# A fused adaLN block on one core: the quantizer's slots by a table, and the engines' lists of steps placed anew

## What is computed

```python
mod = (silu(c) @ wmod)                      # shifts and scales sa, ca, ga, sb, cb, gb per batch
h = layernorm(x) * (1 + ca) + sa
x = x + ga * attn(h, Wq, Wk, Wv, ...)       # decayed sums over all 1024 rows of a batch, per head
h = layernorm(x) * (1 + cb) + sb
gate = fp4(h) @ fp4(w_gate).T
y    = fp4(h) @ fp4(w_up).T
f = silu(gate) * y                          # 352 columns
x = x + gb * (fp4(f) @ fp4(w_down).T)

def fp4(x):                                 # blocks of 16 along the last dimension
    scale = max(max(abs(xb)) / 6, 1e-12)
    return nearest(GRID, abs(xb / scale)) * sign(xb) * scale
```

## Time and profile before

| what | value |
|---|---|
| median of 3 runs | 199.48 us (198.5 to 200.17) |
| the profiled execution's own time | 199.69 us |
| its span (first to last instruction) | 197.7 us |
| PE busy | 184.5 us (93%), 1022 matmuls |
| DVE, POOL busy | 161.1 us, 160.9 us (81% each) |
| ACT busy | 133.8 us (68%) |
| granted TensorE clock | 1.00 in every stretch |

### The profile page before, as it was taken

One profiled execution on the slowest core, in us unless ns is written; L12 is line 12 of the kernel. 1 busy time (PEld: TensorE's weight loads), 2 busy tenths in 40 slices (PEclk: granted clock), 3 DMA queues, 4 the chain that ended last, 5 costly groups with the idle time before them and its releaser, 6 DMA issues.

```text
span 197.7 us, 3626 instructions
## 1 busy us (share of the span) xinstructions
PE 184.5 (93%) x1022; PEld 144.9 (73%) x1022; DVE 161.1 (81%) x408; ACT 133.8 (68%) x319; POOL 160.9 (81%) x205
## 2 busy tenths in 40 slices
PE   4999999999999999999799999999889997979984
PEld 3756588778878779689479869769676684765873
DVE  3849969868877999999989999999989876876830
ACT  2369999968687899858925765765565575555442
POOL 6985999989978998997799989896969799473550
PEclk9999999999999999999999999999999999999999
DMA  5981005100000000000000000001000010010001
GB/s 145 279 218 37 0 3 171 46 0 3 0 0 2 0 0 5 0 0 3 27 3 0 27 3 27 28 0 30 28 27 0 3 53 27 0 56 0 28 27 53
DMA packets 11650, 6.71 MB, mean 34 GB/s; under 512 B 1704, under 2 KB 11372, under 8 KB 11504
## 3 DMA queue, kind: packets, MB, share of 16 engines
q1 hardware_dynamic: 11320, 6.36, 11.4%
q10 hardware_dynamic: 312, 0.13, 0.2%
HBM read 4.39 MB, written 2.11 MB: 33 GB/s over the span
## 4 chain that ended last, share of the span: by engine, by line
PE 45%; POOL 24%; issue 15%; DVE 10%; ACT 3%; DMA 1%; POOLq 0%; DVEq 0%; ACTq 0%
PE pa L1085 9%; POOL q_r L498 6%; POOL q_o L510 6%; PE pa L1189 4%; PE pv L1021 4%; PE pg L1119 4%; PE pv L1191 4%; POOL kw L454 3%; DVE q_x L958 3%; PE pv L1153 3%; PE pa L1213 2%; POOL rstdb L477 2%; POOL xn L411 2%; PE pa L1200 2%; DVE q_r L961 2%
## 5 line engine op out<-in xcount | busy, mean ns | idle before, releaser
L498 POOL TENSOR_TENSOR q_r<-q_x,q_rs 128x960 f32<-128x960 f32 (+2 forms) x18 | 29.5, 1640 | 10.8 <-DVE q_rs L950 10.3
L510 POOL TENSOR_TENSOR q_o<-q_r,q_sp 128x960 f32<-128x960 f32 (+2 forms) x18 | 29.5, 1641 | 7.4 <-DVE q_r L961 7.2
L1189 PE MATMUL pa<-guT,hqT 128*128 128x352 f32 x64 | 25.2, 475 | 2.5 <-ACT hqT L708 2.4
L1213 PE MATMUL pa<-wdg,fqT 128*128 128x128 f32 x192 | 27.3, 278 | 0.1
L717 ACT ACTIVATE sgl<-pa 128x352 f32<-128x352 f32 x32 | 14.6, 462 | 15.0 <-PE pa L1189 12.0
L1213 PEld LDWEIGHTS pa<-wdg,fqT 128*128 128x128 f32 x192 | 24.0, 192 | 1.0 <-ACT fqT L725 0.4
L1191 PE MATMUL pv<-guT,hqT 128*128 128x352 f32 x64 | 24.3, 461 | 0.3 <-DVE x_all L913 0.3
L1085 PE MATMUL pa<-wcat,hT 128*128 128x368 f32 x64 | 23.7, 504 | 0.0
L702 ACT ACTIVATE q_A<-q_r 128x960 f32<-128x960 bf16 (+2 forms) x18 | 16.0, 888 | 11.4 <-DVE q_r L961 6.2
L958 DVE SCALAR_TENSOR_TENSOR q_x<-q_A,q_r 128x960 f32<-128x960 f32 (+2 forms) x18 | 18.5, 1029 | 4.6 <-ACT q_A L702 4.6
L454 POOL TENSOR_TENSOR kw<-kg,cw 128x256 f32<-128x256 f32 x32 | 19.6, 636 | 1.8 <-DVE cw L864 1.8
(11 more groups left out here) (157 smaller groups left out, 452.0 us busy)
## 6 DMA issues: line engine op xcount, KB each, us to landing
out_dram<-x_all SPq DMA_DIRECT2D x16, 128.0 KB, 1.8
x_all<-in_L_attn_x_dram SPq DMA_DIRECT2D x3, 512.0 KB, 5.4
...
```

Of the source, the lines that this page charges most:

```text
L498: g.tensor_tensor(blocks(q_r[:, s % 2, c]), blocks(q_x[:, s % 2, c]), spread(q_rs[:, s % 2, n]), ALU.mult)\
L510: g.tensor_tensor(blocks(q_o[:, s % 2, c]), blocks(q_r[:, s % 2, c]), spread(q_sp[:, s % 2, n]), ALU.mult)\
L1189: te.matmul(bank_a(("G%d" % k, i))[:, 0:I], lhs, guT[:, 0, :], start=True, stop=True)\
L1213: last = te.matmul(t[:, k * D:(k + 1) * D], fqT[:, (2 * i + k) % 4, ch * P:(ch + 1) * P], wdg[:, b % 2, ch, :], start=False, stop=(ch == 2))
```

## The change

The slots are now given by a table: for each slot the norm it carries, the pair whose FFN rows it carries, and which of the pair's two tiles. Slots 0 to 14 are as before. Slot 15 has norm 15 alone (before: with FFN rows 13), 16 has FFN rows 13, 17 has FFN rows 14, 18 has the first tile of FFN rows 15 and 19 the second. Waits and buffer numbers are taken from the table; F1 on DVE and F3 on PE wait for each tile's slot by itself. All four lists of steps are written anew.

```diff
-Q_NORM, Q_FFN = 4, 6
+SLOTS = [(0, None, ()), (1, None, ())] + [(i, i - 2, (0, 1)) for i in range(2, 15)] + [(15, None, ()), (None, 13, (0, 1)), (None, 14, (0, 1)), (None, 15, (0,)), (None, 15, (1,))]
...
-        def quant_span(s):
-
-            lo = 0 if s - Q_FFN >= 0 else QF0
-            return slice(lo, QCOLS if s - Q_NORM < PAIRS else QF0), slice(lo // BLOCK, (QCOLS if s - Q_NORM < PAIRS else QF0) // BLOCK)
-
-        def nth(s):
-            return s - Q_NORM + 1
+        slot_n = {norm: k for k, (norm, _, _) in enumerate(SLOTS) if norm is not None}
+        slot_f = {(ffn, t): k for k, (_, ffn, tiles) in enumerate(SLOTS) for t in tiles}
+
+        def quant_span(k):
+
+            norm, ffn, tiles = SLOTS[k]
+            lo = tiles[0] * I if tiles else QF0
+            hi = QCOLS if norm is not None else (tiles[-1] + 1) * I
+            return slice(lo, hi), slice(lo // BLOCK, hi // BLOCK)
+
+        def nth(k):
+            return k + 1
...
             def Q(s):
-                if nth(s) < 1:
-                    return
                 r, (c, n) = s % 2, quant_span(s)
-                if s - Q_FFN >= 0:
-                    dve.wait_ge(S["v_free"], slot_v[("U1", s - Q_FFN)] + 1)
-                if s - Q_NORM < PAIRS:
-                    dve.wait_ge(S["h2"], s - Q_NORM + 1)
+                norm, ffn, tiles = SLOTS[s]
+                if ffn is not None:
+                    dve.wait_ge(S["v_free"], slot_v[("U%d" % tiles[-1], ffn)] + 1)
+                if norm is not None:
+                    dve.wait_ge(S["h2"], norm + 1)
...
             def F1(i):
-                r = (i + Q_FFN) % 2
-                if i + Q_FFN - 2 >= Q_NORM:
-                    dve.wait_ge(S["q_q"], nth(i + Q_FFN - 2))
-                for k in range(2):
+                for k in range(2):
+                    r = slot_f[(i, k)] % 2
+                    if slot_f[(i, k)] >= 2:
+                        dve.wait_ge(S["q_q"], nth(slot_f[(i, k)] - 2))
...
             def F3(i):
-                pe.wait_ge(S["q_o"], nth(i + Q_FFN))
-                for k in range(2):
+                for k in range(2):
+                    pe.wait_ge(S["q_o"], nth(slot_f[(i, k)]))
                     t = bank_a(("FT%d" % k, i))
```

Of the lists, the last line of POOL's before and after:

```diff
-        L1:14 QO:17 L1:15 QR:18 QR:19 QO:18 QO:19 QR:20 QR:21 QO:20 QO:21""",
+        O3:15 QR:14 L1:15 QO:14 QR:15 QR:16 QO:15 QR:17 QO:16 QO:17 QR:18 QR:19 QO:18 QO:19""",
```

More of the change, by code:

```diff
@@ L501, in QO @@
             def QO(s):
[L502 to L503 removed]
                 c, n = quant_span(s)
                 pool.wait_ge(S["q_q"], nth(s))
[L506 to L509 removed]
+                if s >= 2:
+                    norm, ffn, tiles = SLOTS[s - 2]
+                    if norm is not None:
+                        pool.wait_ge(S["a_full"], slot_a[("HQT", norm)] + 1)
+                    if ffn is not None:
+                        pool.wait_ge(S["a_full"], slot_a[("FT%d" % tiles[-1], ffn)] + 1)
                 g.tensor_tensor(blocks(q_o[:, s % 2, c]), blocks(q_r[:, s % 2, c]), spread(q_sp[:, s % 2, n]), ALU.mult)\
@@ L1176, in N4 @@
             def N4(i):
-                pe.wait_ge(S["q_o"], nth(i + Q_NORM))
+                pe.wait_ge(S["q_o"], nth(slot_n[i]))
                 t = bank_a(("HQT", i))
                 for k in range(2):
-                    last = te.transpose(t[:, k * D:(k + 1) * D], q_o[:, (i + Q_NORM) % 2, QF0 + k * D:QF0 + (k + 1) * D], ident[:, :])
+                    last = te.transpose(t[:, k * D:(k + 1) * D], q_o[:, slot_n[i] % 2, QF0 + k * D:QF0 + (k + 1) * D], ident[:, :])
                 last.then_inc(S["a_full"], 1)
@@ L1199, in F3 @@
                         o = k * I + CH[ch]
-                        last = te.transpose(t[:, ch * P:(ch + 1) * P], q_o[:, (i + Q_FFN) % 2, o:o + P], ident[:, :])
+                        last = te.transpose(t[:, ch * P:(ch + 1) * P], q_o[:, slot_f[(i, k)] % 2, o:o + P], ident[:, :])
                     last.then_inc(S["a_full"], 1)
```

96 lines of the change are left out of this document (44 added, 52 removed).

## The result

The changed kernel takes 200.25 us (median of 20 executions, 198.65 to 205.98) for 198.34 us before (20 executions, 197.34 to 200.17). The ratio of the comparable executions is 1.0055, interval 1.0028 to 1.0082: about 1.1 us slower, where the sum of the forecast's terms was 0.4 us faster. So the two medians above are not compared. The profiled execution after took 199.86 us, its span is 197.7 us.

A forecast was written before the change was run, and what follows sets the result against it. TensorE, 93% busy, was taken to bound the kernel, waiting only for the quantizer's round trip. 199.69 + 0.0 - 1.0 + 0.0 + 0.6 = 199.3 us, less 0.21 us for the median: 199.1 us; range 196.6 to 201.9 us.

The forecast's parts named there:

- -1.0 us in the middle: 60 to 163 us: PE's waits behind DVE's slow cw come back, 1.0 us of at most 1.04 us.
- +0.6 in the tail: From 163 us on: the new lists, replayed, lose 0.6 us; range -0.6 to +1.8 us.
- The step on cw: GD:3 ahead of L1:5 on ACT lets cw precede POOL's q_o, taking near 0.42 us instead of 2.06 us.
- 0 for these: Middle: the other 3.1 us of PE's waits before 163 us change by 0, from -1.5 to +0.5 us.
- Rival 1: 60 to 163 us: nearly all of PE's 4.12 us of waits comes back, set at 3.2 us, 196.9 us; chance 0.28.
- The front, 0.0 forecast: 0 to 60 us: PE has only 0.12 us of waits and the fillers stay, so 0.0 us; lower bound -0.1 us.
- Rival 2: Front: ACT's block ahead of PX:11 becomes PE's wait, 202.1 us, or 201.1 us with cw's gain; chance 0.19.
- The replay: Tail: new lists stepped from slot 12's last multiply; POOL's last multiply ends at about 193.75 us, before 192.01 us.
- only one tile's transposes, its copy and half of F4 are left, about 1.9 us: Tail's end: from POOL's last multiply to the last matmul's end about 1.9 us, where before took 3.0 us.
- So norm 15 alone brings 0.2 us: Tail: slot 15 with norm 15 only ends about 180.2 us, before 180.40 us, so a gain of 0.2 us, not more.
- the lower end of the tail's range: Tail: a win of 0.6 us if F4:12 did not hold up F1:15.

The follow-up runs named there:

- middle_fix: h_middle with two steps moved back: QT:10 ahead of O3:13 on DVE, QA:10 ahead of F4:5 and F3:6 on ACT; ratio to before 0.9967.
- h_middle: The kernel before with only the middle of the lists (about 80 to 145 us) new; front, tail and slots as before; ratio to before 1.0006.
- h_front: The kernel before with only the front of the four lists (to about 75 us) new; middle, tail and slots as before; ratio to before 0.995.
- t_half: The changed kernel with the last pair's transposes and down projection issued tile by tile on PE; ratio to before 1.0058.
- t_f1: The changed kernel with F1:15 moved ahead of F4:12 on PE and ACT; ratio to before 1.0066.
- norm_only: The changed kernel without the cut: norm 15 alone in its slot, rows 15 whole in one slot; ratio to before 1.0159.
- split_only: New front and middle, before's tail and slots, but the last slot cut in two and the steps around it ordered as in the changed kernel; ratio to before 1.0158.

## Why the prediction was wrong, point by point

**The sign.** Forecast were -1.0 us in the middle and +0.6 in the tail, -0.4 in all. Behind W3 the trace has -0.83 and +1.17, so +0.3, and the ratio has +1.1. So two terms that were too good by 0.2 and 0.6 us turned the sign, and 0.8 us came from where the forecast had no term.

**The middle, -1.0 us forecast, -0.8 measured.** The step on cw held in every part: it comes first now, takes 0.43 us, and PE's three waits from 94 to 99 us are gone (it is busy all the 5.50 us from 94.00 us on, for 4.49 before). "0 for these" was the mistake beside it, hidden by a second one of the other sign. I had looked at the order of F1:10 and not at slot 10: O3:13 ahead of QT:10 on DVE and QA:10 behind F4:5 and F3:6 on ACT make it 1.2 us later (74.7 us, and 73.5 in middle_fix), and Q:11 ahead of L1:12 escapes nmrb's 1.14 us. In h_middle, without that last step, nothing of cw's gain is left. Rival 1 did not come: PE's waits from 60 us to the end of slot 12's last multiply went from 4.37 to 3.95 us, where it wanted under 1.5.

**The front, 0.0 forecast.** h_front is 1.0 us faster than before, but by cw's gain, which it has in another way. Rival 2 (ACT's block) didn't come: PE's 0.57 us of waits between 2.5 and 60 us lie nearly all at 4.2 us, behind a load, and from 30 us on there are none.

**The tail, +0.6 us forecast, +1.2 measured.** The replay held up to the last multiply: F1:15 comes 21.2 us behind slot 12's last multiply for 19.9 before (1.3 later; 1.2 forecast), and the last multiply ends 30.6 us behind slot 12's end (30.5 forecast, 28.8 before). The step that failed is the last term: "only one tile's transposes, its copy and half of F4 are left, about 1.9 us". From the last multiply's end to the end of ACT's copy it takes 195.44 - 192.64 = 2.8 us for the forecast 2.3, and 3.5 before. Both tiles' transposes stand ahead of F4:15, whose two halves run from 193.08 to 195.02 us; and t_half shows that the other order doesn't give the half us back, since the first half of F4 isn't ready early enough. "So norm 15 alone brings 0.2 us" was near for slot 15 itself, whose last multiply ends 17.3 us behind slot 12's for 17.2 before, and wrong as the price of the edit: alone it costs 2.9 us. And the lower end of the tail's range, 0.6 us won if F4:12 did not hold up F1:15, had no ground: in t_f1 F1:15 starts 1.1 us sooner and nothing is won.

**The rest, 0.8 us.** After's profile is 0.3 us behind before's from W3 on, but its ratio says 1.1 us. Part of the difference lies outside the span, and the times and spans of all executions show it. Time less span is 2.2 us on the mean over after's eleven comparable executions, and 1.8 to 1.9 us over before's in the sets it was run in beside the experiments. The six kernels with norm 15 in a slot of its own have 2.1 to 2.4 us (t_half 2.2, norm_only 2.1), the others with before's slots, h_front among them, 1.7 to 1.8, and split_only 1.8. So 0.3 to 0.4 us goes with that slot, though no run shows what takes it; the forecast had no term for it. The other 0.4 us lies before W3, where single profiles differ by 1 us and PE reached W3 earlier in this profile (67.14 for 67.51 us), or in executions that no profile shows, and stays open.

**The basis.** The forecast of 199.1 us was built on 199.69 us of one execution and a median of three. Over 20 executions before takes 198.34 us, 1.1 us under that median; on that base the same terms give 197.9 us. So the 199.1 us lies nearer to the 199.4 us that the ratio gives than its terms deserve: that is luck.

**Two slips in the working.** Each of the two more slots costs an instruction in eight places, not seven, and DVE's rounding costs (860 - 420) / 448 = 0.98 ns per column, not 1.05; the 0.52 us for 352 columns is worked out from 0.98. Neither moves the sum.
